# Local attention in a stack of layers: the mix of values without a half of zeros, and scores, mask, maxima and mix each in two halves with transposes between them

## The reference, cut to what matters

```python
DIM = 128; DEPTH = 6; HEADS = 16; DIM_HEAD = 64; WINDOW = 32; QK_SCALE = 8.0
def local_attention(q, k, v):                       # b, h, n, d
    ...
    bk2, bv2 = (look(bk), look(bv))                 # the window before, then the own one: 64 keys
    ...
    mask = (it < jb) | (it > jb + w) | (jb == -1)
    sim = jnp.einsum('bhwie,bhwje->bhwij', bq, bk2) * QK_SCALE
    sim = jnp.where(mask, -jnp.finfo(sim.dtype).max, sim)
    attn = jax.nn.softmax(sim, -1)
    out = jnp.einsum('bhwij,bhwje->bhwie', attn, bv2)
    return out.reshape(b, h, n, d)
for i in range(DEPTH):
    x = attn_layer(shift_tokens(x), Wqkv[i], q_scale[i], k_scale[i], Wo[i]) + x
    x = ffn_layer(shift_tokens(x), ...) + x
```

## Time and profile before

| what | before |
|---|---|
| median of 3 runs | 1909.38 us |
| all runs | 1898.79, 1910.66, 1909.38 us |
| profiled execution: time, span of the trace | 1898.89 us, 1897.1 us |
| TensorE clock granted, mean over the span | 0.927 of full speed |
| busy: PE, DVE, ACT, POOL | 1606.4 (85%), 1250.9 (66%), 989.3 (52%), 762.1 (40%) us |
| scores L1542: records, busy | 6144, 78.0 us |
| mix L1616: records, busy | 3072, 94.3 us |
| scores of the first and the last tile start at | 572.0, 1414.7 us |

### The profile page before, as it was taken

How to read it: one execution, slowest core, us unless ns; L and a number is a source line. 1 busy time by engine, 2 the same in 40 slices (tenths; PEclk the granted TensorE clock), 3 DMA queues, 4 the chain that set the end, 5 groups by cost and what they waited for, 6 DMA issues and landing times.

```text
span 1897.1 us, 42488 instructions
## 1 busy us (share of the span) xinstructions
PE 1606.4 (85%) x17121; PEld 1091.3 (58%) x17121; DVE 1250.9 (66%) x2351; ACT 989.3 (52%) x1861; POOL 762.1 (40%) x1082
## 2 busy tenths in 40 slices
PE   3005476999878999999999999999987999999999
PEld 1002264676645666656666666666664677677676
DVE  6846694212957878878878778888864666666211
ACT  1034133333335667756767566666654776677332
POOL 0000030100357676776776667766740333334000
PEclk6556797899978999999999999999999999999999
DMA  3000002010032323322323232332230000000111
GB/s 111 19 6 0 3 1 63 22 35 15 1 108 52 92 74 81 84 71 70 93 73 80 76 77 64 92 83 60 57 87 1 1 1 1 1 1 1 34 34 34
DMA packets 74572, 88.23 MB, mean 47 GB/s; under 512 B 22994, under 2 KB 42936, under 8 KB 74346
## 3 DMA queue, kind: packets, MB, share of 16 engines
q1 hardware_dynamic: 73562, 85.28, 17.3%
q10 hardware_dynamic: 816, 0.24, 0.1%
HBM read 35.21 MB, written 2.34 MB: 20 GB/s over the span
## 4 chain that ended last, share of the span: by engine, by line
PE 60%; DVE 27%; issue 6%; ACT 4%; DVEq 1%; DMA 1%; POOL 0%; ACTq 0%; POOLq 0%; SPq 0%
PE PS L1412 8%; PE PS L1132 6%; PE PS L1123 6%; PE PS L1664 4%; PE PS L2162 4%; DVE st_t L1456 3%; PE PS L2119 3%; PE PS L1542 3%; PE PS L2141 3%; DVE st_r L1448 3%; DVE st_ss L1461 3%; DVE st_den L1581 2%; PE PS L1779 2%; PE PS L1616 2%; PE PS L1521 2%
## 5 line engine op out<-in xcount | busy, mean ns | idle before, releaser
L1490 POOL TENSOR_TENSOR st_r<-st_r,st_t 128x512 f32<-128x512 f32 x192 | 243.8, 1276 | 193.0 <-DVE st_t L1456 193.0
L1412 PE MATMUL PS<-st_wqkv,st_xs 128*128 128x512 f32 x576 | 306.1, 616 | 14.3 <-DVE st_t L1456 8.8
L2266 POOL TENSOR_SCALAR la_p<-la_p,la_rden 128x589 f32<-128x589 f32 x64 | 112.9, 1764 | 229.8 <-DVE la_rden L2285 229.8
L1448 DVE TENSOR_TENSOR st_r<-PS,st_rot 128x512 f32<-128x512 f32 x192 | 129.2, 673 | 102.7 <-ACT st_sqh L1432 101.9
L1507 POOL TENSOR_TENSOR st_r<-st_r,st_gy 128x512 f32<-128x512 f32 x192 | 195.1, 1049 | 3.8
L1191 ACT ACTIVATE m_h<-PS 128x512 f32<-128x512 f32 x128 | 76.1, 598 | 139.9 <-PE PS L1123 139.9
L2279 DVE TENSOR_REDUCE la_nmx<-PS 128x1 f32<-128x589 f32 x128 | 92.7, 766 | 84.8 <-PE PS L2124 84.8
L1432 ACT ACTIVATE st_sqh<-PS 128x512 f32<-128x512 f32 x192 | 114.6, 597 | 54.9 <-PE PS L1412 53.8
L2231 ACT ACTIVATE la_p<-PS,la_nmx 128x589 f32<-128x589 f32 x128 | 95.1, 748 | 82.0 <-DVE la_nmx L2279 81.9
L1216 DVE SCALAR_TENSOR_TENSOR m_y<-PS,m_g,m_y 128x128 f32<-128x128 f32 x112 | 31.5, 344 | 159.6 <-PE PS L1132 159.6
L806 POOL MEMSET l_s<- 128x144 f32 x2 | 0.4, 222 | 329.2 <-DVE x L648 215.9
(11 more groups left out here) (311 smaller groups left out, 3490.0 us busy)
## 6 DMA issues: line engine op xcount, KB each, us to landing
st_vv<-st_v SPq DMA_DIRECT2D x744, 64.0 KB, 2.0
st_wqkv<-in_st_wqkv SPq DMA_DIRECT2D x18, 512.0 KB, 4.2
m_w<-in_m_w SPq DMA_DIRECT2D x32, 256.0 KB, 3.1
st_wo<-in_st_wo SPq DMA_DIRECT2D x6, 512.0 KB
st_w<-in_st_w SPq DMA_DIRECT2D x6, 341.0 KB
la_wc<-in_la_wc SPq DMA_DIRECT2D x1, 1344.0 KB, 6.9
ca_blocks<-in_blank SPq DMA_DIRECT2D x1, 1280.0 KB, 7.0
st_qks<-in_st_qks SPq DMA_DIRECT2D x6, 128.0 KB, 4.4
```

The costliest lines, as they stand in the source:

```text
L1412: pe.matmul(PS[:, 2 + m % 2, :], self.xs[:, b, P * t:P * t + P], self.wqkv[:, l % 2, k, 512 * half:512 * half + 512], start=True, stop=Tru ...
L1448: dve.tensor_tensor(h3(self.r[:, t % 2, c, :]), h3(ps), self.rot[:, k, 0, t, :].unsqueeze(1) .broadcast_to([P, 8, D2]), ALU.mult)
L1490: pool.tensor_tensor(r, r, self.t2[:, c % 2, :], ALU.add).then_inc(self.added, 1)
```

## The change

Four things are altered, all in the stack.

The values tile loses its zero blocks (vv has half the columns), and the mix is made by matmuls with 64 rows and 64 columns, one for each head, pair and window: 64 a tile in place of 32. Its result now lies by head e in bank e, as the scores do, and dve_out reads it in that order. The mix is issued in two halves of four pairs; between them stand the transposes of quarter 1 of q and k (and at t = 0 the variance). The second up-projection at t = 1 now comes after the second half.

The scores are issued in two halves, by e: first all 32 matmuls of head 0 of the pairs, then all of head 1. Between them stands pe_turn_o(T - 1, 1). The mask is written by two instructions and the maxima are taken by two, one for each e, with semaphore counts to match.

The diff:

```diff
--- before.py
+++ after.py
@@ -1262,7 +1262,7 @@
             self.kT = s("kT", [P, 8, WIN + S])
             self.v = s("v", [P, 2, INNER])
 
-            self.vv = s("vv", [P, 8, 2, INNER // 2])
+            self.vv = s("vv", [P, 8, INNER // 2])
             self.e = s("e", [P, 8, 2, 2 * WIN])
             self.pT = s("pT", [P, 8, P])
             self.mx = s("mx", [P, 16])
@@ -1339,7 +1339,7 @@
             source = 4 * T + w - (1 - h)
             rows = slice(64 * e + WIN * h, 64 * e + WIN * h + WIN)
             block = slice(WIN * (source % 4), WIN * (source % 4) + WIN)
-            sp.dma_start(self.vv[rows, 4 * (T % 2) + w, e, :],
+            sp.dma_start(self.vv[rows, 4 * (T % 2) + w, :],
                          self.v[block, source // 4 % 2, 512 * e:512 * e + 512]).then_inc(signal, 16)
 
         def crossed(self, T):
@@ -1530,20 +1530,20 @@
             act.activation(dst, src, ACT.Copy).then_inc(self.r_evac, 1)
 
 
-        def pe_scores(self, pe, T):
+        def pe_scores(self, pe, T, e):
 
             t = T % self.TILES
-            pe.wait_ge(self.r_evac, 4 * T + 4)
-            pe.wait_ge(self.masked, T + 2)
+            if e == 0:
+                pe.wait_ge(self.r_evac, 4 * T + 4)
+            pe.wait_ge(self.masked, 2 * T + 2 + e)
             for c in range(8):
                 for w in range(4):
-                    for e in range(2):
-                        k = P * t + WIN * w
-                        mm = pe.matmul(PS[WIN * w:WIN * w + WIN, e, D2 * c:D2 * c + D2],
-                                       self.qT[64 * e:64 * e + 64, c, WIN * w:WIN * w + WIN],
-                                       self.kT[64 * e:64 * e + 64, c, k:k + 2 * WIN],
-                                       start=False, stop=(c == 7), skip_group_check=True,
-                                       tile_position=(64 * e, WIN * w))
+                    k = P * t + WIN * w
+                    mm = pe.matmul(PS[WIN * w:WIN * w + WIN, e, D2 * c:D2 * c + D2],
+                                   self.qT[64 * e:64 * e + 64, c, WIN * w:WIN * w + WIN],
+                                   self.kT[64 * e:64 * e + 64, c, k:k + 2 * WIN],
+                                   start=False, stop=(c == 7), skip_group_check=True,
+                                   tile_position=(64 * e, WIN * w))
             mm.then_inc(self.scores, 1)
 
         def act_mask(self, act, T):
@@ -1554,17 +1554,19 @@
                 act.wait_ge(self.masked, 1)
             else:
                 act.wait_ge(self.on_ready, T)
-            act.activation(PS[:, 0:2, :].rearrange("p e (c k) -> p (e c) k", c=8),
-                           self.wmask[:, min(t, 1), :].unsqueeze(1).broadcast_to([P, 16, 2 * WIN]), ACT.Copy)\
-               .then_inc(self.masked, 1)
+            for e in range(2):
+                act.activation(PS[:, e, :].rearrange("p (c k) -> p c k", c=8),
+                               self.wmask[:, min(t, 1), :].unsqueeze(1).broadcast_to([P, 8, 2 * WIN]), ACT.Copy)\
+                   .then_inc(self.masked, 1)
 
         def dve_max(self, dve, T):
 
             heads = lambda a: a.rearrange("p (e c) -> p e c", e=2)
-            dve.wait_ge(self.scores, T + 1)
             ps = PS[:, 0:2, :].rearrange("p e (c k) -> p e c k", c=8)
-            dve.tensor_reduce(heads(self.mx[:, :]), ps, X, ALU.max).then_inc(self.mx_ready, 1)
-            dve.wait_ge(self.mx_ready, T + 1)
+            for e in range(2):
+                dve.wait_ge(self.scores, 2 * T + 1 + e)
+                dve.tensor_reduce(self.mx[:, 8 * e:8 * e + 8], ps[:, e, :, :], X, ALU.max).then_inc(self.mx_ready, 1)
+            dve.wait_ge(self.mx_ready, 2 * T + 2)
             if T > 0:
                 dve.wait_ge(self.p_turned, 2 * T)
                 dve.wait_ge(self.den_ready, T)
@@ -1603,29 +1605,33 @@
             act.activation(self.pT[:, 4 * half:4 * half + 4, :], PS[:, 4 + half, :].rearrange("p (c n) -> p c n", c=4),
                            ACT.Copy).then_inc(self.p_evac, 1)
 
-        def pe_mix(self, pe, T):
+        def pe_mix(self, pe, T, half):
 
             u, t = divmod(T, self.TILES)
-            pe.wait_ge(self.p_evac, 2 * T + 2)
-            pe.wait_ge(self.vshift[t], (u + 1) * self.OWN)
-            if t:
-                pe.wait_ge(*self.crossed(T))
-            for c in range(8):
+            pe.wait_ge(self.p_evac, 2 * T + 1 + half)
+            if half == 0:
+                pe.wait_ge(self.vshift[t], (u + 1) * self.OWN)
+                if t:
+                    pe.wait_ge(*self.crossed(T))
+            for c in range(4 * half, 4 * half + 4):
                 for w in range(4):
                     g = slice(WIN * w, WIN * w + WIN)
-                    mm = pe.matmul(PS[g, c // 4, P * (c % 4):P * (c % 4) + P], self.pT[:, c, g],
-                                   self.vv[:, 4 * (T % 2) + w, :, D2 * c:D2 * c + D2], start=(c % 4 == 0), stop=(c % 4 == 3),
-                                   tile_position=(0, WIN * w), skip_group_check=True)
-            mm.then_inc(self.pv_done, 1)
+                    for e in range(2):
+                        keys = slice(64 * e, 64 * e + 64)
+                        mm = pe.matmul(PS[g, e, D2 * c:D2 * c + D2], self.pT[keys, c, g],
+                                       self.vv[keys, 4 * (T % 2) + w, D2 * c:D2 * c + D2], start=(c == 0), stop=(c == 7),
+                                       tile_position=(64 * e, WIN * w), skip_group_check=True)
+            if half:
+                mm.then_inc(self.pv_done, 1)
 
         def dve_out(self, dve, T):
             dve.wait_ge(self.pv_done, T + 1)
             dve.wait_ge(self.rden_ready, T + 1)
             if T > 0:
                 dve.wait_ge(self.o_turned, 2 * T)
-            dve.tensor_tensor(self.on[:, :, :, :].rearrange("p (b c) e d -> p b (c e) d", b=2),
-                              PS[:, 0:2, :].rearrange("p b (h d) -> p b h d", h=8),
-                              self.rden[:, T % 2, :].rearrange("p (b h) -> p b h", b=2).unsqueeze(3)
+            dve.tensor_tensor(self.on[:, :, :, :].rearrange("p c e d -> p e c d"),
+                              PS[:, 0:2, :].rearrange("p e (c d) -> p e c d", c=8),
+                              self.rden[:, T % 2, :].rearrange("p (c e) -> p e c", e=2).unsqueeze(3)
                               .broadcast_to([P, 2, 8, D2]), ALU.mult).then_inc(self.on_ready, 1)
 
         def pe_turn_o(self, pe, T, half):
@@ -1807,11 +1813,13 @@
                 if lead and not fresh:
                     self.pe_proj(pe, T + 2, 0)
                 if here:
-                    self.pe_scores(pe, T)
+                    self.pe_scores(pe, T, 0)
+                if past:
+                    self.pe_turn_o(pe, T - 1, 1)
+                if here:
+                    self.pe_scores(pe, T, 1)
                 if fresh:
                     self.pe_proj(pe, T + 2, 0)
-                if past:
-                    self.pe_turn_o(pe, T - 1, 1)
                 if lead:
                     self.pe_proj(pe, T + 2, 1)
                 if past:
@@ -1832,13 +1840,15 @@
                 if turn:
                     self.pe_turn_r(pe, T + 1, 0)
                 if here:
-                    self.pe_mix(pe, T)
-                if end_of is not None:
-                    self.pe_up(pe, end_of, 1)
+                    self.pe_mix(pe, T, 0)
                 if norm_of is not None:
                     self.pe_var(pe, norm_of)
                 if turn:
                     self.pe_turn_r(pe, T + 1, 1)
+                if here:
+                    self.pe_mix(pe, T, 1)
+                if end_of is not None:
+                    self.pe_up(pe, end_of, 1)
                 if lead:
                     self.pe_proj(pe, T + 2, 4)
                 if norm_of is not None:
@@ -1957,7 +1967,7 @@
         def pool(self, pool):
 
             for k, what in enumerate((self.xs[64:P, :, 0:1], self.xf[64:P, 0:1], self.kT[:, :, 0:WIN],
-                                      self.vv[:, 0:4, :, :], self.vv[:, 4:8, :, :])):
+                                      self.vv[:, 0:4, :], self.vv[:, 4:8, :])):
                 pool.memset(what, 0.0).then_inc(self.set_up, 1)
                 pool.wait_ge(self.set_up, k + 1)
             pool.wait_ge(self.c_in, 32)
```

## The result

The changed kernel takes 1942.12 us in the median of 4 runs (1933.56 to 1947.62), the kernel before 1907.41 of 4 (1898.79 to 1910.66): ratio 1.018, interval 1.0142 to 1.0217. The forecast was 1929 (1.010), its range 1903 to 1949. The profiled execution took 1939.09 us. First its page: span, TensorE's busy time, the queue that brings instructions, and the two lines of small matmuls.

The account below looks back on a forecast made before the run. It took the bound as a chain: TensorE's lap from projection 0 to projection 2, then VectorE's lap. Terms gave +1.77 us a pass, 21.2 for twelve, less 1.5: +20 on 1898.89, scaled to 1929; range 1903 to 1949.

Parts of the forecast that it names:

- Scores +0.64 a step: Scores burst in two halves over four tiles each: 1.17 us a half, 2.34 for two, against 1.70 today.
- A: Stack step at T % 4 = 3: scores on the deciding chain, mix not; forecast 0.64 us longer.
- first rival: Scores halves: weights load only when a round's tiles finish, +0.48 a half, 1965 us; half hidden, 1947; together chance 0.22.
- Entries that cost nothing: Rival for small-tile bursts: no new entry cost, scores pair +0.34, mix -0.51, 1915 us; chance 0.24 together with lower-bound halves.
- D +0.64: Stack step at T % 4 = 2: chain passes the scores, so their split makes it 0.64 us longer.
- B +0.64 - 0.21: Stack step at T % 4 = 0: chain passes scores and mix, so +0.64 and -0.21 us both count.
- C +0.06: Stack step at T % 4 = 1, mostly feed-forward: neither scores nor mix counts, only two maxima for one, +0.06 us.
- The mix -0.21: Mix without zeros in two halves: 0.91 us each, 1.82 against 2.03, counted only at T % 4 = 0.
- The copy ahead of the stack, -1.5: VectorE's copy before the first projection: shorter GpSimd fills cut it from 1.98 to 0.43 us, -1.5 once.

Follow-up runs that it names:

- ScalarE swap: Changed kernel with the copy of the turned output put ahead of both copies of v at T % 4 = 2 alone; 1933.71 us, ratio 1.0146.
- mix in one piece: Changed kernel with both halves of the mix back to back, ahead of the variance, at T % 4 = 0 alone; 1939.22 us, ratio 1.0181.
- mix_whole: Kernel before with the mix in 64-row pieces, both halves back to back in the old place, old scores, mask and maxima; 1936.37 us, ratio 1.0165.

## Why the prediction held, and where it was wrong

- **The time.** 1942 lies in the range and on the side that I thought likelier by a little, but 13 us above the forecast, and by a sum that is only half right. That it lies in the range is in part luck: the ledger below has 9.6 us that the first four steps gave back and of which the sum knew nothing; without them the time would be near 1952, above the range (an estimate, 1942 + 9.6).
- **Scores +0.64 a step.** Right in kind and size. First to last start 0.88 for 0.85, A +0.58; the rule of the Trainium skill (TensorE: Matmul & The Clock Gate, Part 3), by which a weight load overlaps matmuls only from another row group, did not show here either: loads that took turns alone would give a half of 1.33 (0.85 + 0.48, the first rival), and this trace has 0.88 with one row group.
- **The first rival, slower rounds,** gives 1947 or 1965 and so comes nearer to the time, but its mechanism is refuted by the 0.88. **Entries that cost nothing** are too: A would have grown by 0.34.
- **D +0.64** measured +1.2. The term that failed took the longer burst for the whole and put what stands behind the scores in D at nothing: projection 0 stands behind the second half in D, so its first copy of v comes late, and ScalarE does it ahead of the second copy of the turned output. The ScalarE swap shows 0.5 to 0.6 of it.
- **B +0.64 - 0.21** measured +0.9. The failed step is "VectorE's output step ... covered". I read the cover in A, where it had over a microsecond; in B four more matmuls of variance stand between the halves. The mix in one piece gives 0.9 of it back in the shortest step, the mix's halves alone cost B 0.8, and the scores' halves alone nothing (17.11): so it is the turn that B pays for, and the scores' +0.64 is absorbed there.
- **C +0.06** measured -0.06, where the +0.06 of the maxima can't be told from nothing. With the old mix C's median is 22.76, half a microsecond more; that stays open.
- **The mix -0.21.** Its bursts are short as forecast (0.64 for 0.61), and with no turn between them so are the shortest steps (B 16.79 for 17.07, -0.28), but the term missed what the doubled count costs: 12.0 us more of stops in the changed kernel, 25.2 with the old scores. I wrote that the instruction count is why the halved columns don't halve the time, and priced it by TensorE's rate alone, not by the supply of instructions. The row was at hand: the earlier trace rows has 14.4 us of "issue" on the scores, and the forecast did not ask what it was.
- **The copy ahead of the stack, -1.5.** The copies of VectorE after and GpSimd's fills:

```profile
541.12 0.69 DVE L236 TENSOR_TENSOR st_y<-xc,PS 128x512 f32<-128x512 f32 x1 [0.17 <-PE PS L194]
541.73 0.42 DVE L1923 COPY xn<-x 128x512 f32<-128x512 f32 x1
```

```profile
536.34 3.67 POOL L1971 MEMSET st_vv<- 128x2048 f32 x2
```

The copy takes 0.42 beside 1.98, as forecast. But it starts 0.84 later, since what is ahead came later in this execution, and the first scores start 0.6 earlier (571.4 for 572.0). The term is right for the copy and off by 0.9 for the start.

**The ledger of the stack,** +32 us (841.5 to 873.6). Tiles 4 to 45 are 10.5 passes of 75.6 for 71.6, +42: 27 are the order (10.5 x 2.6; 18.6 forecast), and 15 are left for the stops, which are 17 us more there (25.6 for 8.7). The first four steps are 63.5 for 73.1, -9.6: before had three of its seven stops there (7.2 us), after one of 1.3; where the other 3.7 come from is open. Outside the stack the profile grew by 8 (1055.6 to 1063.7). The twelve profiles, whose work there is the same, spread from 1055.6 to 1070.8 with no relation to the change, so those 8 us I can't give to it. One place shows in windows of the stretch behind the stack: 1450 to 1480 has a granted clock of 0.90 before and 0.77 after, and in this window the two kernels don't do the same work.

**What stays open.** That TensorE waits for a packet of instructions is inferred from four things: the remainder by 256, packets of 256 instructions, stops that end 2.15 to 3.07 us after the packet ahead began while no place is passed sooner than that, and stops that move when places are shifted. A packet's own transfer takes about 1.1 us; what the rest of the 2.5 us is, no view shows, nor what sets when a packet begins. And the costs are not additive: the two parts alone cost 13.6 + 31.6 us of stack, together 32.1. The steps with no stop do add up (2.2 + 0.3 a pass, together 2.5, in medians); the stops don't (6.6 us less in one part, 25.2 more in the other, 12.0 more together). That is half of the 13.1 us; the other half is open.

## What to carry to other kernels

Count instructions as a cost of their own: where TensorE runs 128 short matmuls and their weight loads in a microsecond or two, ask what a doubled count does to the supply, not only what the columns save. Idle time "for nothing that the profile shows" inside a burst that waits for nobody is worth a look at the instruction queue in just that window; here moving the code by a few dozen instructions was worth 0.5 to 0.8%, and none of the reorderings tried here beat the kernel before. And when an instruction is moved, follow the queue of each engine that evacuates it in every kind of step, not in the one whose rows are at hand.

## Hardware behaviour that I had not expected

- TensorE stopped 0.3 to 3.2 us (start to start) inside bursts of small matmuls, each time at remainder 193 or 194 by 256 of its instructions, and went on 2.15 to 3.07 us after a 16 KB packet of instructions had begun (229 stops in twelve traces). The old kernel lost 16 us to seven such stops, mix_whole (the mix without zeros in one go) 53.8 to 29.
- Four tiles of one row group with 64 columns take 0.88 us from first to last start of 64 records, 16 rounds of 0.055, half of the 0.107 of the old mix's 128 columns, so their weight loads add nothing that shows; eight tiles take 0.64.
- Two fills by GpSimd slow a copy of VectorE beside them from 0.42 to 1.98 us.
